# First step of a two-layer graph kernel: the order of its set-up products, relu statistics, second h and skip additions

## The chip, the cores and the metric

The kernel runs on one core of one Trainium2 chip, in one launch for the whole batch. The metric is the time of one execution on the device in microseconds; of several executions the median is taken.

## The reference

Sixteen batches of x (512 x 256) with their adjacency (512 x 512) go through two residual blocks. Cut to what matters:

```
h  = relu(layernorm(x))
H  = (adj != 0)                       # incidence
Be = 1 / column counts of H;  Dn = 1 / (H @ first row of adj)
r  = relu(Dn * H @ (Be * H^T @ (h @ W1^T)) + b1)
r  = layernorm(r) * gamma + beta
x1 = x + h + Dn * H @ (Be * H^T @ (r @ W2^T)) + b2

X  = relu(layernorm(x1))
e  = leaky_relu(sj + si + ab);  A = adj * exp(e), rows divided by their sums   # sj, si: (X @ Wv + bv) @ aw
H3 = X @ Wk[0] + A @ (X @ Wk[1]) + A @ A @ (X @ Wk[2]) + sum of bk
out = x1 + relu(H3)
```

## The kernel before

Every value that TensorE multiplies is split into a high and a low part (`_hi`, `_lo`). A product of two such values takes three matmuls, one with a 0/1 incidence matrix takes two. A tile is 128 rows, so a batch has four of everything (TI = 4).

Five engines run lists written out by hand, and only semaphores tie them. `run_steps` calls each engine's `step(s)` for k = -1, 0, 1, then in a loop, then for the last ones. Step k holds block 1 of batch k (from `u` on), block 2 of batch k-1 and its last products, and the opening (`h`, incidence, `m`) of batch k+1. Step -1 has only the opening of batch 0. Step k = 0 has no batch before it, and the set-up of the weights runs in it: the gamma-weighted `W2`, the row `c0_row` of beta, the column products of Wv and aw, the parts of Wk. The change lies in step 0 and the opening of step 1.

The names, in the order of step 0:
- TensorE: `u`, then the `z` tiles, with `mean_of_gamma` between (L811) and `mean_of_beta` after them (L801). `products_of_weights` (L815) follows: twelve tiny matmuls that wait for `su_rows`, the rows that GpSimd makes at L509. Then 16 transposes of relu (L981), the 48 matmuls of y, which wait for `dv_ntlo` of each tile, `g_stage` (L1023) for the current batch, which needs all four `y_lo`, `m_stage` (L1013) for the next batch, which needs its four `h_lo` and incidences, and the out products (L1093).
- ScalarE: `relu` (L556), `w2_hi`, the reads of the products' PSUM (L625 to L630), high parts of the transposes `nt_hi` (L680), `y_hi` (L709), `h_of` (L566) for the second batch, `g_hi`, `m_hi`, `wk_hi`.
- VectorE, in `first_step` (L1431): `z_tile`, `stats_r` and `norm_r` (relu statistics, aggregated), `w2_lo` (L1458), `incidence` (L1128), `lo_of_nt` (L1252), `stats_x` and `means_of_x` (statistics of the second x), `y_lo` (L1271), `shift_of_x`, `g_tile`, `h_lo_of`, `sums` (L1115), `inct_of`, `m_parts` (L1295), `x1_tile` (L1354). Then comes `second_step_to_y2` (L1561).
- GpSimd: in `setup` (L495) the skip rows of batch 0, x + b2 (L501) and then + h (L505), rows for the products (L509 to L513). In step 0 the skip rows of batch 1 (L441), `rs_r` (L453) and `rs_x` (L383), the powers that the norms need, `h_hi`, `g_lo` (L470), the h addition for batch 1 (L399), `wk_lo` (L479), which waits for all four x1 tiles.
- SP issues the loads. `adj_sb` holds two of four adjacency tiles. In step 0 SP waits for two incidence tiles of batch 1 (`dv_inc` at TI + 2, L334) and then loads the other two (L275), which `incidence(2)` waits for.

A wait stands in an engine's list like an instruction: all that is behind it waits as well.

```
sp.wait_ge(su_gam, 1)
load_adjt(s)
sp.wait_ge(dv_inc, TI + 2)
load_adj(s, 1, 1)
load_x(s)
```

Of the kernel before, what the change touches and what calls it, by code (L numbers as in the profile page):

```python
# [53 lines left out]
def at(s, ahead, tile=3):  # L54

    return s.k4 + (4 * ahead + tile + 1)
# [37 lines left out]
def build(nc, x, adj, adj_t, w1_t, b1, gamma, beta, w2_t, b2, wv_t, bv, aw, ab, wk, bk, out):  # L94
    NB, C, D = x.shape
    HID = w1_t.shape[1]
    TI = C // P
# [6 lines left out]
    with ExitStack() as ctx:  # L104
# [3 lines left out]
        def sem(name):  # L108
            return ctx.enter_context(nc.semaphore(name))
# [101 lines left out]
        ld_at0 = [sem(f"ld_at0_{c}") for c in range(TI)]  # L211
        ld_b2, ld_gb = sem("ld_b2"), sem("ld_gb")
        su_ones, su_pool, su_rows, su_pe, su_c = (sem(n) for n in ("su_ones", "su_pool", "su_rows", "su_pe", "su_c"))
        su_w2, su_wk = sem("su_w2"), sem("su_wk")
        su_w1hi, su_w2hi, su_wkhi = (sem(n) for n in ("su_w1hi", "su_w2hi", "su_wkhi"))
        su_w1lo, su_w2lo, su_wklo = (sem(n) for n in ("su_w1lo", "su_w2lo", "su_wklo"))

# [137 lines left out]
        def _(pool):  # L355
# [30 lines left out]
            def h_hi_of(s, t):  # L386
                pool.tensor_scalar(h_hi[:, t, 0:D], h_f[:, t, :], 1.0, 0.0, ALU.mult,  # L387
                                   ALU.add).then_inc(h_hi_made, 1)
# [27 lines left out]
            def step(s):  # L416
# [16 lines left out]
                                           ALU.pow).then_inc(po_rsx, 2)  # L433
                elif s.k != 0 and (s.next or s.here):
                    rs_of_x(s)
                if s.next and s.k != -1:

                    wait(pool, ld_x, dma_at(s, 0))
                    wait(pool, dv_x1, at(s, -1))
                    for c in range(TI):  # L440
                        pool.tensor_tensor(skip[:, o, c, :], xin[:, c, :], b2_row[:, :], ALU.add).then_inc(po_xb, 1)  # L441
                if s.k not in (-1, 0):
                    h_parts(s)
                if s.prev2 and s.prev:
# [9 lines left out]
                if s.prev2 and s.prev:  # L454
                    for t in range(TI - 1, TI):
                        wait(pool, ac_v, at(s, -2, t))
                        pool.tensor_tensor(x1[:, q, t, :], y10[:, t, D:], x1[:, q, t, :], ALU.add).then_inc(po_out, 1)
                if s.k == 0:
                    rs_of_x(s)
                    wait(pool, pe_m, at(s, 0))  # L460
                    for t in range(TI):
                        pool.wait_ge(ac_hf, TI + t + 1)
                        h_hi_of(s, t)
                if s.prev and s.here:
                    wait(pool, dv_alo, at(s, -1))
                    y0_of(s)
# [5 lines left out]
                if s.k == 0:  # L472
                    pool.wait_ge(dv_inct, 2 * TI)
                    for t in range(TI):
                        skip_of(s, t)
                    pool.wait_ge(su_wkhi, 1)
                    wait(pool, dv_x1, at(s, 0))
                    for d in range(TD):
                        pool.tensor_tensor(wk_lo[:, d, :], wk_f[:, d, :], f32(wk_hi[:, d, :]),  # L479
                                           ALU.subtract).then_inc(su_wklo, 1)  # L480
# [14 lines left out]
            def setup():  # L495

                pool.wait_ge(dv_dn, TI)
                pool.wait_ge(ld_b2, 16)
                for c in range(TI):
                    pool.wait_ge(ld_x0[c // 2], 16)  # L500
                    pool.tensor_tensor(skip[:, 0, c, :], xin[:, c, :], b2_row[:, :], ALU.add).then_inc(po_xb, 1)  # L501
                for c in range(TI):
                    pool.wait_ge(po_xb, c + 1)
                    pool.wait_ge(ac_hf, c + 1)
                    pool.tensor_tensor(skip[:, 0, c, :], skip[:, 0, c, :], h_f[:, c, :],  # L505
                                       ALU.add).then_inc(po_skip, 1)
                pool.wait_ge(ld_w, 16 * n_w)
                for c in range(TD):
                    last = pool.tensor_scalar(bv_f[:, c, :], ones_f, bv_c[:, c:c + 1], 0.0, ALU.mult, ALU.add)  # L509
                last.then_inc(su_rows, 1)  # L510
                pool.tensor_tensor(bk_row[:, :], bk_f[:, 0, :], bk_f[:, 1, :], ALU.add).then_inc(su_rows, 1)
                pool.wait_ge(su_rows, 2)
                pool.tensor_tensor(bk_row[:, :], bk_row[:, :], bk_f[:, 2, :], ALU.add).then_inc(su_rows, 1)  # L513
                pool.wait_ge(su_rows, 3)
# [5 lines left out]
        def _(act):  # L520
# [16 lines left out]
            def step(s):  # L537
# [64 lines left out]
                def to_scores():  # L602
# [18 lines left out]
                    relu(3)  # L621
                    xt_of(1)
                    if s.k == 0:
                        act.wait_ge(su_pe, 1)
                        act.activation(c_e[:, :], ps1[:, 2, 0:1], ACT.Identity, bias=ab_c[:, :]).then_inc(su_c, 1)  # L625
                        act.activation(c0_row[:, :], ps1[:, 0, 0:D], ACT.Copy).then_inc(su_c, 1)
                        act.activation(wk_f[:, :, D:D2], ps1[:, 1, 0:2 * TD].rearrange("p (a b) -> p a b", a=TD),
                                       ACT.Copy).then_inc(su_wk, 1)
                        act.wait_ge(su_c, 1)
                        act.activation(c_e[:, :], ps1[:, 2, 1:2], ACT.Identity, bias=c_e[:, :]).then_inc(su_c, 1)  # L630
                    if s.k != 0:
                        h_of(3)
                    relu_v(0)
# [117 lines left out]
                exp(3)  # L751
                y10_out(3)
                if s.k == 0:
                    for t in range(TI):
                        y_hi(t)
                    act.wait_ge(su_w2lo, 1)
                    for t in range(TI):
                        h_of(t)
                    g_hi_of()
                    m_hi()  # L760
                    act.wait_ge(su_wk, 1)
                    act.activation(wk_hi[:, :, :], wk_f, ACT.Copy).then_inc(su_wkhi, 1)
                    return
# [25 lines left out]
        def _(pe):  # L789
# [11 lines left out]
            def mean_of_beta():  # L801

                pe.wait_ge(su_gb, 2)
                for c in range(TH):
                    mm(ps1[:, 0, 0:D], beta_f[:, c, :], w2_f[:, c, :], c == 0, c == TH - 1)

            def mean_of_gamma():

# [6 lines left out]
            def products_of_weights():  # L815

                pe.wait_ge(su_rows, 1)
                for d in range(TD):
                    for c in range(TD):
                        mm(ps1[:, 1, 2 * d:2 * d + 2], wv_f[:, c, col(d)], aw_c[:, c, :], c == 0, c == TD - 1)  # L820
                for c in range(TD):
                    last = mm(ps1[:, 2, 0:2], bv_f[:, c, :], aw_c[:, c, :], c == 0, c == TD - 1)
                last.then_inc(su_pe, 1)
                pe.wait_ge(su_pool, 4)

            def step(s):
# [83 lines left out]
                        last.then_inc(pe_z, 1)  # L910
                if s.k == 0:
                    mean_of_beta()
                    products_of_weights()
                if s.prev:

                    if s.here:
# [68 lines left out]
                if s.here:  # L985

                    if s.k == 0:
                        pe.wait_ge(su_w2lo, 1)
                        pe.wait_ge(su_c, 3)
                    for t in range(TI):  # L990
                        wait(pe, dv_ntlo, at(s, 0, t))
                        if s.prev:
# [77 lines left out]
                if s.k == -1:  # L1070
                    m_first()
                elif s.k == 0:
                    g_stage()
                    m_stage()
                elif s.next:
                    m_stage()
# [25 lines left out]
        def _(dve):  # L1102
            def step(s):
# [327 lines left out]
                def first_step():  # L1431
# [19 lines left out]
                                                        ps1[:, 3, 0:D], ALU.mult, ALU.subtract)  # L1451
                    last.then_inc(su_w2, 1)
                    z_tile(2)
                    stats_r(0)
                    z_tile(3)
                    stats_r(1)
                    dve.wait_ge(su_w2hi, 1)
                    dve.tensor_tensor(w2_lo[:, :, :], w2_c[:, :, :], f32(w2_hi[:, :, :]), ALU.subtract).then_inc(su_w2lo, 1)  # L1458
                    incidence(0)
                    incidence(1)  # L1460
                    lo_of_nt(0)
                    stats_r(2)
                    lo_of_nt(1)
                    stats_r(3)
                    for _ in norm_r():
                        pass
                    lo_of_nt(2)
                    for t in range(TI):
                        stats_x(t, 1)
                    means_of_x(0, TI)  # L1470
                    lo_of_nt(3)
                    y_lo(0)
                    incidence(2)
                    y_lo(1)
                    y_lo(2)
                    shift_of_x(0, TI)
                    y_lo(3)
                    incidence(3)
                    dve.wait_ge(su_c, 3)
                    g_tile(0)  # L1480
                    h_lo_of(0)
                    g_tile(1)
                    h_lo_of(1)
                    g_tile(2)
                    h_lo_of(2)
                    h_lo_of(3)
                    g_tile(3)
                    sums(0)
                    sums(1)
                    inct_of()  # L1490
                    m_parts()
                    sums(2)
                    sums(3)
                    second = Step(4, 1, 1, NB)
# [66 lines left out]
                def second_step_to_y2():  # L1561
# [9 lines left out]
                    z_tile(0)  # L1571
                    shift_of_part(slice(TI, 2 * TI), 1)
                    z_tile(1)
                    stats_r(0)
                    z_tile(2)
                    shift_of_part(slice(0, TI), 3)
                    z_tile(3)
                    lo_of_xt(0)
                    lo_of_xt(1)
                    incidence(0)  # L1580
                    stats_r(1)
                    lo_of_y2(0)
                    stats_r(2)
# [155 lines left out]
```

## Time and profile before

| | |
|---|---|
| median of three executions | 828.28 us (828.04 to 829.55) |
| the profiled execution, its own time | 827.77 us |
| its span, first to last instruction | 826.0 us |
| TensorE busy | 806.4 us |
| VectorE, ScalarE, GpSimd busy | 640.7, 474.6, 424.8 us |
| mean granted clock of TensorE | 0.995 |

Names of tiles stand without their numbers: `part_a`, `w_hi` and `ps` stand for several. One line (L791) issues all matmuls, so they are told apart by their tiles: `ps<-h_hi,inc` is `m_stage`, `ps<-part_a,inc` is `g_stage`, `ps<-w_hi,part_a` is z or y, `ps<-aw_c,x` are the products of weights, `ps<-wk_hi,xt_hi` is y2. In the timeline `x4` counts merged instructions, and brackets give the idle time of the engine before the first and what ended it. PE is TensorE, PEld its weight load, DVE VectorE, ACT ScalarE, POOL GpSimd, SPq the issues of SP. The granted clock is a share of the full 2.4 GHz: 0.50 is 1.2 GHz.

### The profile page before, as it was taken

To read this page: it belongs to the slowest core of one execution; us is meant where nothing else is said; L and a number is where in the kernel's file an instruction comes from. 1 tells how busy PE (TensorE), PEld (TensorE's weight loads), DVE (VectorE), ACT (ScalarE), POOL (GpSimd) and SP (SyncE) were. 2 spreads that over 40 slices of the span, in tenths; PEclk is the share of its full clock that TensorE was granted. 3 is DMA by queue.
4 is the path that set the end of the run, shared out by engine and by line. 5 is a ranking of instruction groups with operands and counts; after the bars stand their busy time and mean duration, and the time that the engine had idled before them with its cause. 6 is when DMAs were issued, how large, how long until landed. Compare 5 with 4: busy or idle time off the path is not lost.

```text
span 826.0 us, 16648 instructions
## 1 busy us (share of the span) xinstructions
PE 806.4 (98%) x5750; PEld 752.1 (91%) x5750; DVE 640.7 (78%) x1733; ACT 474.6 (57%) x1004; POOL 424.8 (51%) x587
## 2 busy tenths in 40 slices
PE   7998999999999999999999999999999999999997
PEld 5877989999999999989999899999999999899986
DVE  6797888777789787888777788777878877777566
ACT  4348457483755738467482755738366573754654
POOL 2657482735737365472636638364473636542132
PEclk9999999999999999999999999999999999999999
DMA  8411205022130402205031120402204031110000
GB/s 296 124 65 52 90 1 166 2 89 78 34 131 0 158 8 76 89 0 165 0 104 61 59 106 0 164 1 76 89 11 154 0 128 38 52 52 1 26 27 27
DMA packets 39856, 57.83 MB, mean 70 GB/s; under 512 B 2576, under 2 KB 21008, under 8 KB 39824
## 3 DMA queue, kind: packets, MB, share of 16 engines
q1 hardware_dynamic: 39104, 57.42, 21.1%
q8 instruction: 17, 0.28, 0.1%
q14 instruction: 15, 0.12, 0.1%
q10 hardware_dynamic: 720, 0.01, 0.0%
HBM read 49.03 MB, written 8.39 MB: 70 GB/s over the span
## 4 chain that ended last, share of the span: by engine, by line
PE 88%; DVE 2%; POOL 1%; ACT 1%; issue 0%; POOLq 0%; DVEq 0%; ACTq 0%
PE ps L791 83%; PE ps L981 3%; PE ps L926 2%; PE ps L970 1%; POOL p_lo L484 1%; POOL y L406 0%; ACT xl L553 0%; DVE e_sb L1262 0%; DVE y L1157 0%; DVE x L1162 0%; DVE x L1360 0%; DVE xt_lo L1168 0%; DVE a_lo L1638 0%; DVE part_a L1143 0%; DVE y L1312 0%
## 5 line engine op out<-in xcount | busy, mean ns | idle before, releaser
L791 PE MATMUL ps<-w_hi,part_a 128*128 128x256 f32 (+1 forms) x512 | 156.6, 340 | 1.2 <-DVE part_a L1143 0.8
L406 POOL TENSOR_TENSOR y<-y,bk_row 128x256 f32<-128x256 f32 x64 | 56.3, 910 | 190.1 <-DVE a_lo L1268 190.1
L791 PE MATMUL ps<-w_lo,part_a 128*128 128x256 f32 (+1 forms) x384 | 122.7, 319 | 0.0
L791 PEld LDWEIGHTS ps<-w_hi,part_a 128*128 128x128 f32 x512 | 96.3, 188 | 14.5 <-DVE part_a L1143 2.9
L791 PE MATMUL ps<-wk_hi,xt_hi 128*128 128x258 f32 (+1 forms) x256 | 90.1, 352 | 3.7 <-DVE xt_lo L1168 3.3
L791 PE MATMUL ps<-wk_hi,xt_lo 128*128 128x258 f32 (+1 forms) x256 | 87.3, 341 | 0.0
L791 PE MATMUL ps<-wk_lo,xt_hi 128*128 128x258 f32 (+1 forms) x256 | 87.2, 341 | 0.0
L791 PEld LDWEIGHTS ps<-w_lo,part_a 128*128 128x128 f32 x384 | 72.8, 190 | 5.6
L484 POOL TENSOR_TENSOR p_lo<-y,p_hi 128x256 fp32r<-128x256 f32 x64 | 45.5, 741 | 62.5 <-ACT p_hi L728 50.6
L1262 DVE TENSOR_TENSOR e_sb<-e_sb,adjt_sb 128x512 f32<-128x512 f32 x64 | 44.6, 699 | 41.9 <-ACT e_sb L661 41.9
L470 POOL TENSOR_TENSOR xt_lo<-xl,xt_hi 128x256 fp32r<-128x256 f32 x60 | 56.6, 971 | 31.0 <-ACT xt_hi L734 31.0
L728 ACT ACTIVATE p_hi<-y 128x256 fp32r<-128x256 f32 x60 | 23.9, 419 | 84.7 <-DVE y L1312 84.7
L791 PE MATMUL ps<-w_hi,part_b 128*128 128x256 f32 x256 | 72.4, 283 | 0.0
L791 PE MATMUL ps<-p_hi,a_hi 128*128 128x256 f32 x256 | 65.3, 286 | 0.3 <-POOL p_lo L484 0.2
L791 PE MATMUL ps<-y_hi,a_hi 128*128 128x258 f32 x256 | 64.6, 282 | 0.5 <-ACT a_hi L688 0.4
L791 PE MATMUL ps<-inct,part_b 128*128 128x512 f32 x256 | 62.7, 396 | 1.7 <-DVE part_b L1292 1.7
L791 PE MATMUL ps<-y_lo,a_hi 128*128 128x256 f32 x256 | 64.4, 282 | 0.0
L791 PE MATMUL ps<-p_lo,a_hi 128*128 128x256 f32 x256 | 63.9, 281 | 0.0
L791 PE MATMUL ps<-part_a,inc 128*128 128x256 f32 x512 | 62.6, 279 | 0.4 <-DVE part_a L1276 0.4
L791 PE MATMUL ps<-h_hi,inc 128*128 128x258 f32 x256 | 60.3, 283 | 2.6 <-POOL h_hi L387 1.6
L791 PEld LDWEIGHTS ps<-part_a,inc 128*128 128x128 f32 x512 | 61.0, 188 | 0.6 <-DVE part_a L1276 0.6
L721 ACT ACTIVATE part_b<-ps,be 128x256 fp32r<-128x256 f32 x64 | 28.4, 474 | 56.3 <-DVE be L1287 52.2
(157 smaller groups left out, 2527.3 us busy)
## 6 DMA issues: line engine op xcount, KB each, us to landing
adj_sb<-in_adj SPq DMA_DIRECT2D x30, 512.0 KB, 5.8
adjt_sb<-in_adj_t SPq DMA_DIRECT2D x15, 1024.0 KB, 5.3
xin<-in_x SPq DMA_DIRECT2D x15, 512.0 KB, 4.7
out_dram<-x SPq DMA_DIRECT2D x15, 512.0 KB, 3.3
w_row<-in_adj SPq DMA_DIRECT2D x16, 256.0 KB, 3.5
adjt_sb<-in_adj_t SPq DMA_DIRECT2D x4, 256.0 KB, 7.3
e_sb<-in_w_t SPq DMA_DIRECT2D x2, 512.0 KB, 8.5
y<-in_wk SPq DMA_DIRECT2D x3, 256.0 KB, 7.1
```

Source lines behind the costliest of these rows:

```text
L406: pool.tensor_tensor(y10[:, t, D:], y10[:, t, D:], bk_row[:, :], ALU.add).then_inc(po_y0, 1)
L470: pool.tensor_tensor(g_lo[:, t, :], g_f[:, t, :], f32(g_hi[:, t, :]), ALU.subtract).then_inc(po_glo, 1)
L484: pool.tensor_tensor(p_lo[:, t, :], y10[:, t, 0:D], f32(p_hi[:, t, :]), ALU.subtract).then_inc(po_plo, 1)
L721: act.activation(part_b[:, t, 0:D], ps0[:, t, 0:D], ACT.Copy, scale=be[:, o, t:t + 1]).then_inc(ac_m, 1)
L728: act.activation(p_hi[:, t, :], y10[:, t, 0:D], ACT.Copy).then_inc(ac_p, 1)
L791: return pe.matmul(dst, stationary, moving, start=first, stop=last, skip_group_check=True)
L926: last = pe.transpose(ps0[:, t, col(2 * j + d)], xl[:, 2 * t + j, col(d)], ident[:, :])
L970: last = pe.transpose(ps1[:, 0, col(t)], column, ident[:, :])
L981: last = pe.transpose(ps0[:, t, col(c)], r_sb[:, t, col(c)], ident[:, :])
L1262: dve.tensor_tensor(e_sb[:, t, :], e_sb[:, t, :], adjt_sb[:, o, t, :], ALU.mult).then_inc(dv_a, 1)
```

## The change

In step 0:
- TensorE issues `products_of_weights` behind y, ahead of `g_stage`, into banks of ps0 where they stood in ps1, after a wait for the four low parts of the transposes. `m_stage` waits for ScalarE's reads of them. y waits for the row of beta alone.
- ScalarE reads only that row ahead of the high parts of the transposes. The other reads come behind `y_hi(3)`, and `h_of` goes between tiles of `y_hi`.
- VectorE does the four `stats_r` and `norm_r` ahead of `lo_of_nt(0)`, the statistics of x between the low parts, `incidence(0)` and `(1)` behind low parts 2 and 3, `h_lo_of` ahead of the g tiles, and one of the four `sums` ahead of `m_parts` where it was two.
- GpSimd adds h to the skip rows of batch 0 behind `rs_r`, and x + b2 of batch 1 behind `h_hi`. `wk_lo` waits for the sums where it waited for x1.

In step 1 VectorE does `z_tile(3)` ahead of the shift and `stats_r(0)` behind the first incidence.

```diff
@@ -211,7 +211,7 @@
         su_ones, su_pool, su_rows, su_pe, su_c = (sem(n) for n in ("su_ones", "su_pool", "su_rows", "su_pe", "su_c"))
-        su_w2, su_wk = sem("su_w2"), sem("su_wk")
+        su_w2, su_wk, su_bet, su_c0 = sem("su_w2"), sem("su_wk"), sem("su_bet"), sem("su_c0")
         su_w1hi, su_w2hi, su_wkhi = (sem(n) for n in ("su_w1hi", "su_w2hi", "su_wkhi"))
@@ -433,12 +433,15 @@
                     rs_of_x(s)
-                if s.next and s.k != -1:
+                def xb_of_next():
...
                         pool.tensor_tensor(skip[:, o, c, :], xin[:, c, :], b2_row[:, :], ALU.add).then_inc(po_xb, 1)
+                if s.next and s.k not in (-1, 0):
+                    xb_of_next()
                 if s.k not in (-1, 0):
@@ -456,11 +459,17 @@
                 if s.k == 0:
+                    for c in range(TI):
+                        pool.wait_ge(po_xb, c + 1)
+                        pool.wait_ge(ac_hf, c + 1)
+                        pool.tensor_tensor(skip[:, 0, c, :], skip[:, 0, c, :], h_f[:, c, :],
+                                           ALU.add).then_inc(po_skip, 1)
                     rs_of_x(s)
...
                         h_hi_of(s, t)
+                    xb_of_next()
                 if s.prev and s.here:
@@ -474,7 +483,7 @@
                     pool.wait_ge(su_wkhi, 1)
-                    wait(pool, dv_x1, at(s, 0))
+                    wait(pool, dv_hw, at(s, 1))
                     for d in range(TD):
@@ -499,11 +508,6 @@
                     pool.tensor_tensor(skip[:, 0, c, :], xin[:, c, :], b2_row[:, :], ALU.add).then_inc(po_xb, 1)
-                for c in range(TI):
-                    pool.wait_ge(po_xb, c + 1)
-                    pool.wait_ge(ac_hf, c + 1)
-                    pool.tensor_tensor(skip[:, 0, c, :], skip[:, 0, c, :], h_f[:, c, :],
-                                       ALU.add).then_inc(po_skip, 1)
                 pool.wait_ge(ld_w, 16 * n_w)
@@ -621,13 +625,8 @@
                     if s.k == 0:
-                        act.wait_ge(su_pe, 1)
-                        act.activation(c_e[:, :], ps1[:, 2, 0:1], ACT.Identity, bias=ab_c[:, :]).then_inc(su_c, 1)
-                        act.activation(c0_row[:, :], ps1[:, 0, 0:D], ACT.Copy).then_inc(su_c, 1)
-                        act.activation(wk_f[:, :, D:D2], ps1[:, 1, 0:2 * TD].rearrange("p (a b) -> p a b", a=TD),
-                                       ACT.Copy).then_inc(su_wk, 1)
-                        act.wait_ge(su_c, 1)
-                        act.activation(c_e[:, :], ps1[:, 2, 1:2], ACT.Identity, bias=c_e[:, :]).then_inc(su_c, 1)
+                        act.wait_ge(su_bet, 1)
+                        act.activation(c0_row[:, :], ps1[:, 0, 0:D], ACT.Copy).then_inc(su_c0, 1)
                     if s.k != 0:
@@ -751,11 +750,21 @@
                 if s.k == 0:
-                    for t in range(TI):
-                        y_hi(t)
                     act.wait_ge(su_w2lo, 1)
-                    for t in range(TI):
-                        h_of(t)
+                    y_hi(0)
+                    h_of(0)
+                    y_hi(1)
+                    h_of(1)
+                    h_of(2)
+                    y_hi(2)
+                    h_of(3)
+                    y_hi(3)
+                    act.wait_ge(su_pe, 1)
+                    act.activation(c_e[:, :], ps0[:, 2, 0:1], ACT.Identity, bias=ab_c[:, :]).then_inc(su_c, 1)
+                    act.activation(wk_f[:, :, D:D2], ps0[:, 1, 0:2 * TD].rearrange("p (a b) -> p a b", a=TD),
+                                   ACT.Copy).then_inc(su_wk, 1)
+                    act.wait_ge(su_c, 1)
+                    act.activation(c_e[:, :], ps0[:, 2, 1:2], ACT.Identity, bias=c_e[:, :]).then_inc(su_c, 1)
                     g_hi_of()
@@ -802,7 +811,8 @@
                 for c in range(TH):
-                    mm(ps1[:, 0, 0:D], beta_f[:, c, :], w2_f[:, c, :], c == 0, c == TH - 1)
+                    last = mm(ps1[:, 0, 0:D], beta_f[:, c, :], w2_f[:, c, :], c == 0, c == TH - 1)
+                last.then_inc(su_bet, 1)
@@ -817,9 +827,9 @@
                     for c in range(TD):
-                        mm(ps1[:, 1, 2 * d:2 * d + 2], wv_f[:, c, col(d)], aw_c[:, c, :], c == 0, c == TD - 1)
+                        mm(ps0[:, 1, 2 * d:2 * d + 2], wv_f[:, c, col(d)], aw_c[:, c, :], c == 0, c == TD - 1)
                 for c in range(TD):
-                    last = mm(ps1[:, 2, 0:2], bv_f[:, c, :], aw_c[:, c, :], c == 0, c == TD - 1)
+                    last = mm(ps0[:, 2, 0:2], bv_f[:, c, :], aw_c[:, c, :], c == 0, c == TD - 1)
                 last.then_inc(su_pe, 1)
@@ -910,7 +920,6 @@
                     mean_of_beta()
-                    products_of_weights()
                 if s.prev:
@@ -986,7 +995,7 @@
                         pe.wait_ge(su_w2lo, 1)
-                        pe.wait_ge(su_c, 3)
+                        pe.wait_ge(su_c0, 1)
                     for t in range(TI):
@@ -1070,7 +1079,11 @@
                 elif s.k == 0:
+                    pe.wait_ge(dv_ntlo, TI)
+                    products_of_weights()
                     g_stage()
+                    pe.wait_ge(su_c, 2)
+                    pe.wait_ge(su_wk, 1)
                     m_stage()
@@ -1451,44 +1464,44 @@
                     z_tile(2)
-                    stats_r(0)
                     z_tile(3)
-                    stats_r(1)
                     dve.wait_ge(su_w2hi, 1)
                     dve.tensor_tensor(w2_lo[:, :, :], w2_c[:, :, :], f32(w2_hi[:, :, :]), ALU.subtract).then_inc(su_w2lo, 1)
-                    incidence(0)
-                    incidence(1)
-                    lo_of_nt(0)
-                    stats_r(2)
-                    lo_of_nt(1)
-                    stats_r(3)
+                    for t in range(TI):
+                        stats_r(t)
                     for _ in norm_r():
                         pass
+                    lo_of_nt(0)
+                    stats_x(0, 1)
+                    stats_x(1, 1)
+                    lo_of_nt(1)
+                    stats_x(2, 1)
+                    stats_x(3, 1)
+                    means_of_x(0, TI)
                     lo_of_nt(2)
-                    for t in range(TI):
-                        stats_x(t, 1)
-                    means_of_x(0, TI)
+                    incidence(0)
                     lo_of_nt(3)
+                    incidence(1)
                     y_lo(0)
+                    shift_of_x(0, TI)
+                    y_lo(1)
                     incidence(2)
-                    y_lo(1)
+                    h_lo_of(0)
                     y_lo(2)
-                    shift_of_x(0, TI)
+                    incidence(3)
+                    h_lo_of(1)
+                    h_lo_of(2)
                     y_lo(3)
-                    incidence(3)
-                    dve.wait_ge(su_c, 3)
+                    h_lo_of(3)
+                    dve.wait_ge(su_c0, 1)
                     g_tile(0)
-                    h_lo_of(0)
                     g_tile(1)
-                    h_lo_of(1)
                     g_tile(2)
-                    h_lo_of(2)
-                    h_lo_of(3)
                     g_tile(3)
+                    inct_of()
                     sums(0)
+                    m_parts()
                     sums(1)
-                    inct_of()
-                    m_parts()
                     sums(2)
@@ -1571,13 +1584,13 @@
                     z_tile(1)
-                    stats_r(0)
                     z_tile(2)
+                    z_tile(3)
                     shift_of_part(slice(0, TI), 3)
-                    z_tile(3)
                     lo_of_xt(0)
...
                     incidence(0)
+                    stats_r(0)
                     stats_r(1)
```

## Rows read from the trace of the kernel before

**Rows 1.** the page, part 1: engine, busy time, share of the span, instructions.
```profile
PE 806.4 (98%) x5750; PEld 752.1 (91%) x5750; DVE 640.7 (78%) x1733; ACT 474.6 (57%) x1004; POOL 424.8 (51%) x587
```

**Rows 2.** waits of TensorE, 25 to 100 us: in total, times, longest.
```profile
PE ps L791 <- DVE xt_lo L1168: 2.2, 1, 2.2
```

**Rows 3.** timeline of TensorE: start, us, instruction, count, idle time before it.
```profile
30.73 1.05 PE L791 MATMUL ps<-aw_c,x 128*128 128x2 f32 x8 [1.97 <-POOL xl L509]
...
32.09 3.47 PE L981 MATMUL ps<-ident,r_sb 128*128 128x128 f32 x16
35.22 0.56 PE L791 MATMUL ps<-w_hi,part_a 128*128 128x256 f32 x1
...
42.54 3.31 PE L791 MATMUL ps<-part_a,inc 128*128 128x256 f32 x26 [0.38 <-DVE part_a L1276]
46.80 0.36 PE L791 MATMUL ps<-h_hi,inc 128*128 128x258 f32 x1 [0.96 <-DVE h_lo L1384]
...
68.63 0.36 PE L791 MATMUL ps<-wk_hi,xt_hi 128*128 128x258 f32 x1 [2.22 <-DVE xt_lo L1168]
```

**Rows 4.** windows: length, busy us by engine, granted clock, DMA share, GB/s.
```profile
12.00:14.00 2.00, 0.53 (x5) 0.32 (x3) 1.03 (x4) 0.89 (x3) 0.00 (x0) 1.00 1.07 374
32.00:34.00 2.00, 2.00 (x13) 2.00 (x13) 0.33 (x1) 1.45 (x6) 1.92 (x4) 0.58 1.03 381
34.00:36.00 2.00, 2.00 (x12) 2.00 (x11) 2.00 (x4) 1.49 (x3) 1.03 (x2) 0.57 0.79 306
69.00:70.00 1.00, 1.00 (x10) 1.00 (x10) 1.00 (x3) 0.38 (x2) 0.00 (x0) 0.93 0.07 16
73.00:74.00 1.00, 1.00 (x5) 0.83 (x5) 0.73 (x4) 0.83 (x2) 0.92 (x3) 0.87 0.00 0
```

**Rows 5.** timeline of VectorE.
```profile
28.43 1.24 DVE L1458 TENSOR_TENSOR w_lo<-e_sb,w_hi 128x1024 fp32r<-128x1024 f32 x1
...
44.51 0.94 DVE L1384 TENSOR_TENSOR h_lo<-h_f,h_hi 128x256 fp32r<-128x256 f32 x1
...
45.76 0.89 DVE L1384 TENSOR_TENSOR h_lo<-h_f,h_hi 128x256 fp32r<-128x256 f32 x2
...
53.95 0.69 DVE L1122 SCALAR_TENSOR_TENSOR hw<-inc,w_row 128x512 f32<-128x512 f32 x1
...
56.28 1.64 DVE L1360 SCALAR_TENSOR_TENSOR x<-ps,dn,skip 128x256 f32<-128x256 f32 x4
...
65.81 0.69 DVE L1244 BATCH_NORM_STATS2 st_r<-r_sb 128x6 f32<-128x512 f32 x1 [2.00 <-ACT r_sb L559]
...
67.81 1.27 DVE L1168 TENSOR_TENSOR xt_lo<-ps,xt_hi 128x512 fp32r<-128x512 f32 x2
...
73.93 0.15 DVE L1621 COPY si<-ps 128x4 f32<-128x4 f32 x1
```

**Rows 6.** timeline of GpSimd.
```profile
25.79 2.81 POOL L505 TENSOR_TENSOR skip<-skip,h_f 128x256 f32<-128x256 f32 x4
...
58.07 3.35 POOL L479 TENSOR_TENSOR wk_lo<-y,wk_hi 128x770 fp32r<-128x770 f32 x2 [5.07 <-DVE x L1360]
```

**Rows 7.** timeline of ScalarE.
```profile
41.86 2.06 ACT L575 ACTIVATE h_f<-xin,nb_x,rs_x 128x256 f32<-128x256 f32 x4
...
66.21 1.05 ACT L564 ACTIVATE xt_hi<-ps 128x512 fp32r<-128x512 f32 x2
```

**Rows 8.** SP's timeline, and DMA issues one by one: KB, us to landing.
```profile
30.48 0.37 SPq L275 DMA_DIRECT2D adj_sb<-in_adj  x1
...
xin<-in_x SPq DMA_DIRECT2D x1, 512.0 KB, 3.4
...
adj_sb<-in_adj SPq DMA_DIRECT2D x1, 512.0 KB, 4.4
...
adj_sb<-in_adj SPq DMA_DIRECT2D x1, 512.0 KB, 6.2
...
w_row<-in_adj SPq DMA_DIRECT2D x1, 256.0 KB, 3.1
```

## Prediction

> **What bounds the kernel now.** I read the page first. TensorE is busy in 98% of the span [rows 1], so only idle or slowed time of TensorE can be won, and an edit to ScalarE, VectorE or GpSimd counts by when it lets TensorE go on. The list of waits of TensorE between 25 and 100 us comes next: 2.2 us for xt_lo, 2.0 us for POOL's L509, 1.0 us for h_lo, and three smaller ones [rows 2, 3]. From 70 us on TensorE is never idle long enough to be listed, so whatever the first two steps gain or lose reaches the end as it is.
>
> The timeline gives the places [rows 3]: idle 28.8 to 30.7 ahead of the products of weights; h_lo at 46.8; xt_lo 66.4 to 68.6. The granted clock gives a second cost [rows 4]: it is 0.5 from 32.3 to 35.7, and again from 69.9 to 73.3 (3.4 us each, 1.7 us of work lost in each), each time after an idle time of about 2 us. Both stretches follow the two longest waits. An idle time of about 1.7 us near 12.5 us (0.53 us busy in 12 to 14, the clock 1.00 [rows 4]) was followed by no fall.
>
> **Changes around the transposes of relu.** The products of weights (30.73 to 32.09, 1.4 us) go behind y. The relu transposes then follow the means of beta at 28.4. All 16 take 3.5 us at the half clock [rows 3]; the same 16 take 1.75 us at the whole one by half of that. They end at 30.3. ScalarE's copies keep up. TensorE is next held by VectorE, where all four relu statistics and their aggregation now precede the first low part of the transposes.
> VectorE: the last z tile needs TensorE's z of 27.04, so 27.1 to 27.8; w_lo 1.2 to 29.0 [rows 5]; four statistics at 0.6 between starts to 31.4; aggregates 0.4 to 31.8; one low part 0.7: y starts at 32.5 where it was 35.22. w_lo reads two SBUF tensors and now runs beside POOL's two-input bk_row additions (27.9 to 29.4, since POOL's h additions of 2.8 us moved away [rows 6]). Such an operation pays for that: h_lo took 0.94 us for one tile beside POOL's xt_lo, and 0.89 for two when half of the time was free of it [rows 5]. At double length over the shared part w_lo would end at 29.6 and y start at 33.1; below 32.5 nothing goes, since the rest of the list is fixed. I take 32.7. That is 2.5 us early, but it leaves TensorE idle for 2.4 us where it was 1.97: **the stall moves, it does not go**, and the clock can fall again. y takes 5.9 us (48 matmuls 0.12 apart): ends 38.6, or 40.3 with a half clock.
> The Trainium skill ("GPSIMD Engine Reference", section Specifications) says that VectorE instructions with two SBUF inputs, or in a 2-port mode, contend with GpSimd for SBUF. The h_lo rows agree for two inputs; by it the incidence operations too would be longer beside the moved skip additions, which adds at most 0.3 us per pair and stays inside the 32.5 to 33.1 above and the ends below.
>
> **The second h.** On POOL, rs_r needs the aggregates (31.8) and ends at 33.3. The skip additions moved behind it hold POOL for 2.8 us [rows 6] to 36.1, in front of rs_x, which with its addition takes some 1.4: 37.5 to 37.7. VectorE's shift gives 37.9, and ScalarE's first h goes at 38.0; four take 2.0 us [rows 7], with three y_hi of 0.4 between and after them: y_hi(3) at 40.9 to 41.3. Before, h began at 41.86. The four products' reads on ScalarE end by 42.4, under TensorE's work on g. So the second h is about 3 us earlier, but h is no longer what ends last.
>
> **The load behind it.** incidence(0) and (1) of batch 1 went from 29.6 to a place behind low parts 2 and 3. SP waits for them before it loads the second half of adj. Walk VectorE from 32.7: two stats_x, low part 1, two stats_x, the aggregates, low part 2, incidence, low part 3, incidence: 1.4 for four stats, 0.4, three parts 1.8, two incidences 0.7, giving 37.0. The load was issued at 30.48 and is now issued at 37.1. By then the queue is empty: SP issues nothing between the half load and the loads that wait for h. A 512 KB load in front of the queue landed 3.4 us after issue, one directly behind another 4.4, one behind 1.3 MB 6.2 [rows 8]. I take 3.4: it lands at 40.5; 41.5 is the upper end, and 40.2 the lower (3.1, the landing of w_row alone, half the size).
> incidence(2) stands on VectorE ahead of h_lo(0), y_lo(2), incidence(3), h_lo(1), h_lo(2), y_lo(3). All of them wait for this load, and g_stage needs y_lo(3). 40.5, plus two incidences 0.7, two y_lo 0.8 and three h_lo 0.6 to 0.9 each (POOL's next skip additions, 2.8 us, run from 41.3) is 43.8 to 44.7: y_lo(3) at 44.2. Before, TensorE had it at 42.54 [rows 3]. TensorE runs y to 38.6 (or 40.3), the products 1.4, six matmuls of g, and then idles until 44.2, together about 3.5 us in the first case and 2.1 in the second. Its 26 remaining matmuls take 3.2 [rows 3]: m_stage starts at 47.4, before it was 46.80. The 1.0 us wait for h_lo is gone, a longer one for y_lo is in front of it: **+0.6**. Low end 46.9, high end 48.9 (load at 41.5 and slow h_lo).
>
> **To the end of the first step.** g_tile(3) ends at 48.0, inct 49.1, sums(0) 50.0. m_parts begins at 50.0 as before. But three sums follow it, not two: one more is 0.73 [rows 5], and x1, which started at 56.28, starts at 57.0: **+0.7**. If the clock falls in g (likely: long idle, hardly any matmuls ahead of it), m ends 1.2 to 1.5 us later, m_parts waits for its last tile, and x1 starts at 57.9. The out products have both parts of g by 49.2, so they wait for nothing.
>
> **The second step.** POOL's wk_lo (3.35 us) ran 58.07 to 61.42 and kept the norm waiting 0.3 us [rows 6]; it now needs only the sums, goes under x1, and gives **-0.3**. stats_r(0) moved: VectorE idled 2.0 us for its relu at 65.8, with z(2) and z(3) behind it, and xt_lo started at 67.81 though its high part was there at 66.8 (two high parts from 66.21 in 1.05 us) [rows 5, 7]. Now z(2) and z(3) run in that idle time: **-1.0**. y2 starts at 68.63 + 0.7 - 0.3 - 1.0 = 68.0 with no fall in g, 69.0 with one. TensorE idles there 1.2 us, less than the 1.7 us after which no fall came, so I take the second stretch of half clock as gone. This is not worth 1.7 us, because VectorE becomes the limit: xt_lo(0) to si was 5.6 us (68.49 to 74.08) and is 5.3 in the new list (four stats 2.4, four y2_lo 1.4, two incidences 0.7, xt_lo 0.6, si 0.2). TensorE's transposes of si, at 74.48 before, go at 73.3 or 74.3: **-1.2 or -0.2**. After that the order is unchanged, and the list of waits up to 100 us has none of TensorE's there.
>
> **Sum.** -1.2 without a fall in g, -0.2 with it; a fall costs less where idle time covers a piece of the half clock, and I forecast between them, **-0.6**. The profiled execution took 827.77 (span 826.0 and 1.8 around it): 827.2 there. It lies 0.5 below the median of 828.28; against the median the forecast is **827.7**.
>
> **Rivals.**
> (a) The clock stays whole in g and the load lands early: y_lo(3) at 43.6, m at 46.8, sums still three, si 1.8 to 2.2 us early. 826.3. For it: the landing of 3.1 and the 1.7 us idle that passed. Against it: 2 to 3.5 us of idle, in a stretch of almost no matmuls.
> (b) The other side, slower: the second half of adj decides. If it lands 6.2 us after issue, as behind other loads, y_lo(3) comes at 47.0, m at 50.2, x1 at 59.3 (+3.0), si at +1.1, and with a fall in g +2.3: 830.6. It turns slower than now from a landing of about 4.6 us without a fall, 3.6 us with one. Against it: SP has nothing before it in the queue at 37 us.
> (c) The clock falls in y2 as before, in spite of the shorter wait. From y2's start to si is then TensorE's 5.85 us, not VectorE's 5.3: si at +0.4 or -0.6. 828.2.
> (d) The first edit works better than I say: w_lo at 32.5 and the clock whole through y. This changes nothing, as y ends before 40.5 in any case; what the load ends is what counts. It goes with the forecast.
>
> **How the numbers follow.** Forecast 50% (827.0 to 828.4), (a) 23%, (c) 14%, (b) 13%. No change that this kernel's measurement can tell is one within 0.2%, 1.7 us: 826.6 to 829.9. Faster takes (a) and a little of the forecast, 27%; slower most of (b), 12%; same the rest, 61%. The range 825.9 to 829.4 takes in (a), (c), and of (b) the landings up to 5 us; the spread of the runs before (1.5 us) is part of it.
>
> **What would show it.** Right: y starts near 32.7 with about 2.4 us idle ahead; the adj load issued near 37; VectorE idle in front of incidence(2) until 40.5; TensorE's longest wait of the first step for y_lo (L1276) and none for L509 or h_lo; m_stage from 47 to 49; x1 0.7 to 1.6 late; y2 with a whole clock and a small wait for si. Wrong: incidence(2) that doesn't wait (then the first step gains 2 us and the total 2.5), x1 earlier than 56.3, or y2 later than 69.5.

## The result and the profile after

The changed kernel takes 831.86 us (median of six, 830.69 to 832.19) against 827.98 for the kernel before (six runs): ratio 1.0043, 95% interval 1.0032 to 1.0055. It is slower by 3.9 us. The forecast was 827.7, in a range that ended at 829.4. Its profiled execution took 831.99 (span 830.2).

Waits of TensorE between 20 and 110 us, for [rows 2]:

```profile
PE ps L800 <- DVE part_a L1156: 2.6, 2, 2.4
PE ps L800 <- DVE part_a L1289: 2.5, 1, 2.5
PE ps L800 <- DVE part_b L1268: 2.1, 1, 2.1
```

L509 and h_lo are gone from the list, as forecast. The low part of the transposes (L1268) and y_lo (L1289) took their places, as forecast. The first line was not forecast: it is z of batch 1, which waits for u_lo behind x1. TensorE's timeline, for [rows 3]:

```profile
32.67 0.36 PE L800 MATMUL ps<-w_hi,part_a 128*128 128x256 f32 x1 [2.13 <-DVE part_b L1268]
...
44.79 5.87 PE L800 MATMUL ps<-part_a,inc 128*128 128x256 f32 x26 [2.47 <-DVE part_a L1289]
...
50.50 0.28 PE L800 MATMUL ps<-h_hi,inc 128*128 128x258 f32 x1
...
64.34 0.79 PE L800 MATMUL ps<-w_hi,part_a 128*128 128x512 f32 x1 [2.40 <-DVE part_a L1156]
...
73.73 0.36 PE L800 MATMUL ps<-wk_hi,xt_hi 128*128 128x258 f32 x1 [1.20 <-DVE xt_lo L1181]
...
78.67 0.65 PE L979 MATMUL ps<-ident,si 128*128 128x128 f32 x4 [0.43 <-DVE si L1634]
```

The same 26 matmuls of g take 5.87 us where they took 3.31. Windows, for [rows 4]; the granted clock stands ahead of the DMA's two columns:

```profile
44.00:46.00 2.00, 1.21 (x5) 1.21 (x6) 1.51 (x4) 0.00 (x0) 0.92 (x2) 0.50 0.00 0
...
48.00:50.00 2.00, 2.00 (x11) 2.00 (x11) 0.48 (x1) 0.68 (x2) 0.73 (x1) 0.50 0.64 238
50.00:52.00 2.00, 2.00 (x17) 2.00 (x16) 1.30 (x2) 0.42 (x1) 1.01 (x2) 0.88 0.00 0
64.00:66.00 2.00, 1.66 (x4) 1.37 (x5) 2.00 (x6) 0.00 (x0) 0.00 (x0) 0.54 0.00 0
```

The last 26 matmuls of g all run at 1.2 GHz; the six ahead of them ran at the whole clock. The clock falls at 43.7, while TensorE is idle, and is whole again at 50.5: 6.8 us of half clock in one stretch, not 3.4. The first part of z runs at 1.2 GHz too (64.1 to 67.6), and a part of y (33.5 to 36.9). VectorE, for [rows 5]:

```profile
40.37 0.67 DVE L1150 TENSOR_SCALAR inc<-adj_sb 128x512 fp32r<-128x512 f32 x1 [0.56 <-DMA adj_sb<-in_adj]
...
59.30 1.50 DVE L1234 SCALAR_TENSOR_TENSOR dn_t<-dn_t 128x4 f32<-128x4 f32 x1
...
61.77 1.64 DVE L1373 SCALAR_TENSOR_TENSOR x<-ps,dn,skip 128x256 f32<-128x256 f32 x4
```

The line at 59.30 is the "safe total", one of the four-column operations that make the denominators `Dn` ahead of x1. It takes 1.50 us. GpSimd is then in wk_lo, for [rows 6]:

```profile
58.92 3.36 POOL L488 TENSOR_TENSOR wk_lo<-y,wk_hi 128x770 fp32r<-128x770 f32 x2 [2.77 <-DVE hw L1135]
```

Its two subtractions take 1.86 and 1.55 us: the first ends at 60.78, the small operation at 60.80.

### The profile page after: what moved, and what is told of

Same layout as the page of the kernel before. It is cut to its first block, busy times and chain, and to the rows that moved or that the text cites. A ratio compares the mean times of both kernels' runs of the same rounds, so it can differ in the third digit from the quotient of the medians.

```text
span 830.2 us, 16648 instructions
## 1 busy us (share of the span) xinstructions
PE 808.8 (97%) x5750; PEld 754.7 (91%) x5750; DVE 643.2 (77%) x1733; ACT 473.8 (57%) x1004; POOL 425.0 (51%) x587
## 4 chain that ended last, share of the span: by engine, by line
PE 88%; DVE 2%; POOL 1%; ACT 1%; issue 0%; POOLq 0%; DVEq 0%; ACTq 0%
PE ps L800 82%; PE ps L990 3%; PE ps L935 2%; PE ps L979 1%; POOL p_lo L493 1%; POOL y L406 0%; DVE st_r L1257 0%; DVE e_sb L1275 0%; DVE xt_lo L1181 0%; DVE y L1170 0%; DVE x L1175 0%; DVE x L1373 0%; DVE a_lo L1651 0%; DVE y L1325 0%; ACT e_sb L654 0%
## 5 line engine op out<-in xcount | busy, mean ns | idle before, releaser
L1275 DVE TENSOR_TENSOR e_sb<-e_sb,adjt_sb 128x512 f32<-128x512 f32 x64 | 44.2, 692 | 41.8 <-ACT e_sb L660 41.8
L800 PE MATMUL ps<-part_a,inc 128*128 128x256 f32 x512 | 65.4, 287 | 2.5 <-DVE part_a L1289 2.5
L800 PEld LDWEIGHTS ps<-part_a,inc 128*128 128x128 f32 x512 | 63.6, 195 | 2.7 <-DVE part_a L1289 2.7
```

The costliest lines, as they stand in the source:

```text
L800: return pe.matmul(dst, stationary, moving, start=first, stop=last, skip_group_check=True)
L1275: dve.tensor_tensor(e_sb[:, t, :], e_sb[:, t, :], adjt_sb[:, o, t, :], ALU.mult).then_inc(dv_a, 1)
```

## The experiments

All twelve experiments are in one table. Medians are in us; each ratio and its interval are to the executions of the kernel before that there were by then, and not the quotient of the two medians shown. The starts are from each kernel's profile, which shows one execution, not always one near the median. That of e4 is the slowest of its eleven: it had a half clock in u and a longer one in y, which make its starts up to 3.2 us later than without them. That of e3 is the fastest of its five, that of e9 (829.1) one of the slowest of its eleven.

Three theories go through the expectations: (1) the late half load, (2) wk_lo beside VectorE's denominators, (3) the third sum behind m_parts.

```
kernel                                 median  ratio to before         m_stage  x1     si
before                                 828.0   (30 runs)               46.80    56.28  74.48
changed                                831.9   1.0043 (1.0032-1.0055)  50.50    61.77  78.67
e1  early incidence                    830.0   1.0018 (1.0009-1.0027)  48.46    60.02  77.25
e2  wk_lo after x1                     829.9   1.0021 (1.0011-1.0030)  50.04    60.03  76.42
e3  filler in g                        831.7   1.0043 (1.0029-1.0057)  48.08    59.62  75.80
e4  second-step edit alone, on before  827.0   0.9982 (0.9973-0.9991)  50.03    59.52  75.90
e5  wk_lo in pieces                    829.6   one run                 49.97    59.90  76.33
e6  e1 + e2                            828.3   1.0002 (0.9993-1.0012)  49.30    59.20  75.57
e7  e6 + sums as before                828.1   1.0006 (0.9997-1.0015)  48.39    58.45  74.83
e8  statistics after low parts         824.0   0.9958 (0.9945-0.9971)  43.40    54.30  70.68
e9  e2 + e3                            828.0   1.0004 (0.9995-1.0013)  49.47    59.40  75.77
e10 e7 + statistics as before          828.9   1.0017 (1.0008-1.0026)  49.01    59.08  75.46
e11 e7 + skip additions in set-up      826.8   0.9985 (0.9976-0.9994)  46.18    56.24  73.54
e12 e8 + x + b2 behind g_lo            825.2   0.9970 (0.9960-0.9981)  43.48    55.09  71.45
```

### The late half load: e1

```diff
+ incidence(0); incidence(1)      # behind w_lo
  for t in range(TI): stats_r(t)
...
- incidence(0)                    # behind lo_of_nt(2)
- incidence(1)                    # behind lo_of_nt(3)
```

> The changed kernel with incidence(0) and (1) back behind w_lo, ahead of the relu statistics. Theory 1, the late half load of adj is what costs most: SP issues it at 30 instead of 36.8, incidence(2) doesn't wait, y starts 0.7 later (33.4), y_lo(3) comes near 42.5 instead of 44.7, TensorE is hardly idle in g, the clock stays whole there (26 matmuls of g in 3.3 us, not 5.87), m_stage starts near 46, and the time is 3.5 to 4.5 us under the changed kernel's: 827.5 to 828.5. Theory 2, wk_lo on GpSimd beside VectorE's denominators is what costs: at most 1 us is won, 831. Theory 3, the third sum behind m_parts holds everything at x1: under 0.5 us is won.

1.8 us were won, half of what theory 1 said. TensorE's wait for y_lo fell from 2.5 to 0.9 us, but g still took 4.85 us, partly at the half clock, and z still waited 2.7 us and began at the half clock.

### wk_lo beside VectorE: e2 and e5

```diff
- wait(pool, dv_hw, at(s, 1))
+ wait(pool, dv_x1, at(s, 0))     # e2
...
- pool.tensor_tensor(wk_lo[:, d, :], ...)
+ for c in range(0, WX, WX // 5): pool.tensor_tensor(wk_lo[:, d, c:c + WX // 5], ...)   # e5
```

> The changed kernel with wk_lo waiting for the four x1 tiles again, as before. Theory 2: VectorE's safe total (1.50 us in the changed kernel, 0.14 before) is short again, x1 starts 1.35 us earlier, TensorE's idle time ahead of z goes from 2.4 to 1.1 us and the half clock behind it goes: 2.5 to 3 us won, 829. Theory 1: 1.4 us at most, 830.5. Rival, the long safe total has another cause: no change, 831.9.

1.9 us were won. The safe total is 0.14 us again, TensorE's wait at z is 1.1 us, and z has the whole clock.

> The changed kernel with each of the two wk_lo subtractions on GpSimd (770 columns, 1.68 us) cut into five of 154 columns, in the same place of its list. Theory 2a, a VectorE instruction that reads two SBUF tensors stands still until the GpSimd instruction under way has ended: safe total takes at most 0.14 + 0.35 us instead of 1.50, and x1 starts 1.0 to 1.3 us earlier. Theory 2b, both only share bandwidth while they run side by side: safe total stays near 1.5 us, since GpSimd is as busy as before.

VectorE's timeline of e5, then GpSimd's:

```profile
58.76 0.16 DVE L1237 SCALAR_TENSOR_TENSOR dn_t<-dn_t 128x4 f32<-128x4 f32 x1
```

```profile
58.39 4.50 POOL L490 TENSOR_TENSOR wk_lo<-y,wk_hi 128x154 fp32r<-128x154 f32 x10 [2.77 <-DVE hw L1138]
```

GpSimd is as busy at 58.76, in pieces that start 0.45 us apart, and the small operation takes 0.16 us. So theory 2b, a shared rate, is out. Theory 2a fits: in the changed kernel VectorE's instruction ended 0.02 us behind GpSimd's first subtraction, and here it had only a short piece beside it. The expectation put 1.68 us on each subtraction, the half of both; the trace has 1.86 for the first. e5 is one execution, and its 829.6 agrees with e2's 829.9.

### The half clock in g: e3 and e9

```diff
+ if s.k == 0 and t == 0 and i == 2:
+     for _ in range(18): mm(ps0[:, 3, 0:D], inc[:, q, 0, col(0)], part_a[:, 0, 0:D], True, True)
  wait(pe, dv_ylo, at(s, 0, i))
```

> The changed kernel with 18 extra matmuls (0.12 us each, 2.2 us, into a free PSUM bank) where TensorE waits for y_lo in g_stage; they add work and change no result. If the half clock in g is what makes m late: the clock stays 1.00 from 42 on, the 26 matmuls take 3.3 us instead of 5.87, m_stage starts near 48 instead of 50.6, and 2.0 to 2.7 us are won: 829.5. If VectorE's list (statistics, sums, the safe total) ends last anyway: under 0.7 us, 831.5.

The profile shows the clock whole in g and the 26 matmuls in 3.33 us; m_stage started 2.4 us and si 2.9 us earlier. But it is the profile of the fastest of the five executions (829.1), and z kept the whole clock in it behind a wait of 2.67 us, which the changed kernel's z did not behind 2.40. The five went from 829.1 to 833.0 and their median didn't move, so by its time this experiment is inconclusive.

> The changed kernel with wk_lo waiting for x1 and the 18 extra matmuls in the wait of g_stage. With wk_lo alone it took 829.9. If the half clock in g costs what the traces say (5.35 instead of 3.3 us for the 26 matmuls), 1.5 to 2 us more are won: 828.2. If VectorE takes it back at x1 (the filler alone left the median at 831.7, though its profile had g in 3.33 us): 829.5 or more.

828.04 over eleven runs, 1.9 us under e2: the added matmuls made the kernel faster. In its profile y kept the whole clock and ended earlier, so the filler ended 2.0 us ahead of y_lo, and g still took 4.85 us. In e3's profile y had a half clock, and the filler ended 0.5 us ahead of y_lo. So keeping TensorE occupied in this wait is worth about 2 us by e9's time, and not even all of the loss is taken away; e3's median doesn't show it, and why not stays open.

### The second step's edit: e4

```diff
  z_tile(1)
- stats_r(0)
  z_tile(2)
+ z_tile(3)
  shift_of_part(slice(0, TI), 3)
- z_tile(3)
...
  incidence(0)
+ stats_r(0)
```

> The kernel before with the edit of the second step alone: z(3) ahead of the shift, stats_r(0) behind the first incidence. By the prediction: y2 starts 1.0 us earlier (67.6), TensorE's wait for xt_lo is 1.2 us, no half clock behind it, si at most 0.5 to 0.9 us earlier because VectorE's list from xt_lo to si takes 5.3 us: 0.5 to 0.9 us under the kernel before, 827.3. Rival, VectorE's list takes back all of it: 828.0.

1.0 us was won, by the median of eleven executions. This part of the change is good by itself.

### Everything put together: e6 and e7

> The changed kernel with both edits of the first experiments: incidence(0) and (1) behind w_lo, and wk_lo waiting for x1. Each alone won 1.8 to 1.9 us. If they are separate costs, they add up: 828.1, with x1 near 58.3 and TensorE's idle time ahead of z 1.1 to 1.3 us. If both won the same thing (the half clock behind the long idle time ahead of z), 829.5.

828.29: the two costs add up.

```diff
- inct_of(); sums(0); m_parts(); sums(1)
+ sums(0); sums(1); inct_of(); m_parts()     # e7
```

> The one before with VectorE's sums(0), sums(1), inct, m_parts, sums(2), sums(3) in the order of the kernel before. Theory 3, the third sum behind m_parts delays x1 by its 0.73 us: x1 starts 0.5 to 0.8 us earlier than in it, and the time falls by 0.5 to 1.0 us. Rival, m_parts starts later by the sum and nothing is won: within 0.3 us of it.

Nothing certain: 828.12 against 828.29. In the two profiles x1 starts 0.75 earlier, but m_stage was already 0.9 earlier.

### What remains ahead of y and h: e8, e10, e11

```diff
# e8, VectorE, as in the kernel before: stats_r(0) and (1) between the z tiles, incidence(0) and (1),
+ lo_of_nt(0); stats_r(2); lo_of_nt(1); stats_r(3); norm_r(); lo_of_nt(2); 4 stats_x; means_of_x; lo_of_nt(3)
# GpSimd: the h additions of batch 0 back in setup()
# ScalarE
+ y_hi(0); y_hi(1); y_hi(2); h_of(0); h_of(1); y_hi(3); h_of(2); h_of(3)
```

> The changed kernel's products of weights behind y and its second-step edit, with VectorE's relu statistics, incidences and sums in the order of the kernel before, batch 0's skip additions back in GpSimd's set-up, three y_hi ahead of h on ScalarE, h_lo ahead of the g tiles, wk_lo waiting for x1. If moving the products is what is worth having and the statistics ahead of the low parts is what spoils it: y starts at 31.1 with under 1 us of idle time ahead, h starts at 37.3 and m_stage near 43.5 instead of 46.8 before, x1 near 53, and the time is 3 to 4 us under the kernel before: 824.5. If the clock or VectorE's list takes it back as in the changed kernel: 827 to 828.

824.00 (five runs, four of them 823.97 to 824.02): 4 us under the kernel before. Waits of TensorE, then its timeline:

```profile
PE ps L800 <- DVE part_a L1156: 1.4, 2, 1.2
PE ps L800 <- DVE xt_lo L1181: 1.3, 1, 1.3
...
PE ps L800 <- DVE part_a L1289: 0.3, 1, 0.3
```

```profile
31.21 0.36 PE L800 MATMUL ps<-w_hi,part_a 128*128 128x256 f32 x1 [0.68 <-DVE part_b L1268]
...
40.25 3.31 PE L800 MATMUL ps<-part_a,inc 128*128 128x256 f32 x26 [0.30 <-DVE part_a L1289]
```

No wait is over 1.3 us, and the clock is 1.00 throughout this execution.

> The kernel with incidences, wk_lo and sums as before (828.1), with VectorE's relu statistics too as before: two between the z tiles, two between low parts. Skip additions stay behind rs_r. If the statistics ahead of the low parts are the cost: y starts 2.1 us earlier (31.2), no half clock in y, and most of the 4 us between 828.1 and 824.0 is won: 825. If the second h is what ends last: rs_x waits for rs_r and the skip additions (39.1), h_lo and y_lo(3) come at 43 or later, TensorE idles in g with the clock falling, and little is won: 827.5 to 828.5.

828.9, worse than e7. VectorE's and TensorE's timelines of e10 show the second h deciding, as the rival said:

```profile
39.09 0.16 DVE L1195 SCALAR_TENSOR_TENSOR nb_x<-mv_x,rs_x 128x4 f32<-128x4 f32 x1 [2.63 <-POOL rs_x L383]
```

```profile
44.28 4.88 PE L800 MATMUL ps<-part_a,inc 128*128 128x256 f32 x26 [1.33 <-DVE part_a L1289]
```

y started at 31.1, and VectorE then waited 2.6 us for rs_x, which stood behind GpSimd's skip additions.

> The same kernel (828.1) with batch 0's skip additions back in GpSimd's set-up and nothing else. If the 2.8 us of skip additions ahead of rs_x are what makes h and y_lo late: rs_x ends at 36.7 instead of 38.1, y_lo(3) comes 1 to 1.5 us earlier, TensorE is idle in g for 1 us less: 826.5 to 827. If y itself (late by the statistics, and at the half clock) holds y_lo(3): no change, 828.

826.8: 1.3 us under e7. VectorE no longer waits for rs_x, and TensorE has no wait for y_lo, though y started at 33.8 and partly at the half clock. Alone, the statistics' order loses 0.8 us and the skip additions' place wins 1.3. Together, with e8's order on ScalarE and of h_lo, they win 4.1.

### One more step: e12

```diff
- xb_of_next()                    # behind h_hi
+ xb_of_next()                    # behind g_lo
```

> The best kernel so far (824.0) with GpSimd's x + b2 additions of the second batch behind g_lo instead of ahead of it. They ran beside VectorE's h_lo and pushed g_lo (43.9 to 48.6) beside sums and inct, which took 1.17, 1.10 and 1.75 us instead of 0.69, 0.69 and 1.22. If an instruction with two SBUF inputs or a whole inct stands still while a GpSimd instruction runs: h_lo 0.6 us shorter, sums and inct 1 us, x1 1 us earlier, no wait for g_lo (0.6): 823.0. Rival: the load of the third x, which waits for these additions, comes too late for its statistics, or skip comes too late for x1: 824 to 825.5.

825.2, slower by 1.2. h_lo did become shorter (three in 1.28 us, not 1.82) and the wait for g_lo went. But GpSimd's additions then stood beside later sums and the denominators (1.10 and 0.59 us, 0.69 and 0.17 in e8), x1 came 0.8 later, and TensorE's wait at z was 2.75 us instead of 1.21. Moving GpSimd's work moved the stall.

## Why the prediction was wrong

Up to y_lo(3) its times held. y started at 32.67 (forecast 32.7) behind 2.13 us of idle time (2.4), the load was issued at 36.83 (37.1), `incidence(2)` started at 40.37 (40.5), and TensorE had y_lo(3) at 44.79 (44.2). But of VectorE's idle time ahead of `incidence(2)` only the last 0.56 us were the load's: 0.94 us went to rs_x and 1.03 us to y_hi(1) before it. One sum has a slip on which nothing rests: with a half clock in y the idle time in g comes to 1.8 us, not 2.1.

**The step that failed is the sum's two lines on g and on x1.** The prediction saw that the clock could fall in g, gave it one stretch of 3.4 us, a cost of 1.2 to 1.5 us, and then took a value between falling and not. The profile shows 6.8 us of it. The 26 matmuls cost 2.6 us more, and m_stage started at 50.50, not at 47.4 to 48.9. e9 prices a part of it in time: 1.9 us for 18 filler matmuls. Ahead of the fall stand the idle time of 2.5 us, and before it six matmuls of g and the tiny products; no run tells which of them counts.

**The second half of the error is wk_lo.** I gave its move -0.3 us because the work "goes under x1". It went under the safe total, which reads two SBUF tensors: 1.36 us on VectorE's path to x1, then a wait of 2.40 us at z, and a stretch of half clock there. e2: 1.9 us. The prediction had the row for this, h_lo at 0.94 us, and named the contention. It priced it for w_lo, h_lo and the incidences beside the moved skip additions only, and as a slower rate rather than as a stop. Those incidences stayed within its 0.3 us (0.52 and 0.41); the one beside the x + b2 additions took 0.93.

x1 by terms: 61.77 against 57.9, the forecast with a fall in g, is 3.9 late. `inct_of` could start at 51.10, not at 48.0, because the last g tile waits for all of g; the forecast had allowed 0.9 of these 3.1 us, which leaves 2.2. sums(0) held VectorE for 1.2 us beside GpSimd's g_lo and skip additions, where 0.9 was put down: 0.3. The safe total is the last 1.4. From x1 to si the forecast was 0.5 too early: 16.90 us against 16.4. y2 started 12.0 behind x1, not 11.1, and in e2, where z kept the whole clock, x1 to si took 16.39. y2 to si took 4.94 us (5.3 forecast, 5.85 before), the clock stayed whole in y2, and the wait for xt_lo was 1.20 us. In time e4 gives 1.0 us for this edit. In the profiles x1 is 5.5 us later than before and si 4.2.

The third sum was a small matter: e7 could not be told from e6. Rival (b) had the sign and the place, and the wrong price: the load landed 3.5 us after issue as forecast, not 6.2. That its m_stage of 50.2 is close to 50.50 is luck, as it put on the landing what the run lost to the clock. Rival (c) was wrong for this profile, though e11's shows that what it describes occurs. (d) was right that y's start is not what counts there.

What the change was worth: e8 keeps the products of weights behind y and the edit of step 1 and takes 824.0, of which the edit of step 1 is worth 1.0 by e4. e8 differs from the kernel before in more than that: `h_of` between `y_hi` on ScalarE, h_lo ahead of the g tiles, and x + b2 behind `h_hi`. No run moves the products alone, so their share of the other 3.0 us is argued and not shown. The changed kernel spent the gain on four moves: wk_lo ahead of x1, the statistics ahead of the low parts, the skip additions ahead of rs_x, and the incidences behind low parts, with the load that waits for them. What e10 and e11 give alone doesn't add up, since y and the second h must both be early. How much of e8's gain is ScalarE's order was not tried.

## What to carry to other kernels

When a stall is taken away, list what the moved work is now beside and in front of. A four-column operation that costs 0.14 us can cost 1.5 beside a long GpSimd instruction, and an incidence nobody waits for can hold a load that everybody waits for. Price an idle stretch of TensorE at its worst, because the half clock that can follow is paid by the matmuls behind it: 2.6 us here, behind 2.5 us of idle time. Two edits that each shorten one of two parallel paths must be tried together.

## What the runs showed of the hardware

The same idle time can be followed by a fall or not. In the kernel before, 1.72 us ahead of u (near 12.5 us) left the clock whole. In e4, whose code up to there is the same, 1.73 us was followed by a fall:

```profile
14.38 5.86 PE L791 MATMUL ps<-inct,part_b 128*128 128x512 f32 x16 [1.73 <-DVE part_b L1292]
```

```profile
16.00:18.00 2.00, 2.00 (x5) 1.49 (x5) 1.39 (x5) 0.55 (x1) 0.00 (x0) 0.52 1.09 351
```

The same holds ahead of y, where the changed kernel's 2.13 us were followed by a fall and e9's 2.13 us, in the same order of work, were not; and ahead of z, where 2.71 us in e1 were followed by one, 2.67 in e3 and 2.75 in e12 were not. Nor is a shorter idle time safe. In e11 y2 ran at the half clock behind 1.32 us, and took 5.87 us to si:

```profile
67.67 0.36 PE L800 MATMUL ps<-wk_hi,xt_hi 128*128 128x258 f32 x1 [1.32 <-DVE xt_lo L1181]
```

```profile
69.00:71.00 2.00, 2.00 (x11) 2.00 (x11) 1.88 (x5) 1.58 (x4) 0.92 (x2) 0.50 0.00 0
```

So the prediction's reading, that 1.2 us is less than the 1.7 us that passed and so passes too, doesn't hold in general. It also fits that kernels with such idle times have no single time: e4's runs went from 825.6 to 829.2, e3's from 829.1 to 833.0, while e8's five went from 823.97 to 824.91. Of the 30 runs of the kernel before, the four slowest (829.35 to 829.53) are the four with the lowest mean clock, 0.992. The clock doesn't explain all of the spread: the three fastest (826.4 to 826.7) had 0.996, and four with 0.998 took 827.2 to 827.4.

In two traces VectorE's instruction with two SBUF inputs ended with the GpSimd instruction beside it: the safe total at 60.80 and wk_lo's first subtraction at 60.78 in the changed kernel, 59.03 and 59.02 in e1. An operation with one SBUF input can be held as well: in e12 a TENSOR_SCALAR on four columns took 0.59 us and ended at 53.65, GpSimd's last addition at 53.62, against 0.17 us in e8.
